# A mixture-of-experts block on one core: the experts' second layer from plain float32 to three products of split parts

## The reference

```python
T, D, I, E, K, CAP = 4096, 512, 256, 64, 6, 128
idx, w = router(x)                                # 6 of 64 experts for each token
xd = zeros((E, CAP + 1, D)).at[e_flat, slot].set(x[tok])   # up to 128 tokens for an expert
h  = square(relu(einsum('ecd,eid->eci', xd, w1)))          # first layer, 512 -> 256
yd = einsum('eci,edi->ecd', h, w2)                         # second layer, 256 -> 512
y  = zeros((T, D)).at[tok].add(yd[e_flat, slot] * gate)    # added up for each token
out = x + layernorm(shared(x) + y)
```

## Time and profile before

| | us |
|---|---|
| median of the three runs shown | 1407.62 (1406.45 to 1408.04) |
| the profiled execution, its own time | 1404.05 |
| its span | 1402.3 |
| TensorE busy, of the span | 1180.5 (84%) |
| VectorE busy | 794.6 (57%) |
| ScalarE busy | 589.5 (42%) |
| GpSimd busy | 284.0 (20%) |

### The profile page before, as it was taken

One profiled execution on the slowest core, in us unless ns is written; L12 is line 12 of the kernel. 1 busy time (PEld: TensorE's weight loads), 2 busy tenths in 40 slices (PEclk: granted clock), 3 DMA queues, 4 the chain that ended last, 5 costly groups with the idle time before them and its releaser, 6 DMA issues. The chain is left out here.

```text
span 1402.3 us, 15536 instructions
## 1 busy us (share of the span) xinstructions
PE 1180.5 (84%) x5024; PEld 773.5 (55%) x5024; DVE 794.6 (57%) x2013; ACT 589.5 (42%) x993; POOL 284.0 (20%) x278
## 2 busy tenths in 40 slices
PE   5998998989898976598989888999999999999400
PEld 3443443434343434377878776777777677777300
DVE  4689797988797989676767681122212221221036
ACT  3464565665565666432232322333333333333124
POOL 2000010201010102100000001332333333343157
PEclk9998999999999987799999998999999999999755
DMA  8201030202020232342121114987996997788997
GB/s 313 97 0 60 0 120 26 95 30 90 30 90 1 90 124 86 139 169 66 63 94 35 64 35 161 234 223 217 258 241 175 275 237 202 226 241 231 285 226 261
DMA packets 80654, 196.74 MB, mean 140 GB/s; under 512 B 10048, under 2 KB 10176, under 8 KB 79552
## 3 DMA queue, kind: packets, MB, share of 16 engines
q1 hardware_dynamic: 64128, 155.93, 33.0%
q0 software_dynamic: 16448, 39.85, 13.8%
HBM read 143.83 MB, written 51.94 MB: 140 GB/s over the span
## 5 line engine op out<-in xcount | busy, mean ns | idle before, releaser
L474 PE MATMUL bank<-mix_ring,weights 128*128 128x512 f32 x768 | 349.8, 613 | 24.7 <-ACT bank L789 15.8
L474 PEld LDWEIGHTS bank<-mix_ring,weights 128*128 128x128 f32 x768 | 149.4, 197 | 214.3 <-issue 208.2
L1560 DVE TENSOR_TENSOR run_max<-run_max 128x256 f32<-128x256 f32 x64 | 27.2, 425 | 218.2 <-ACT run_max L950 218.2
L1534 DVE TENSOR_TENSOR k_sb<-k_sb 128x512 f32<-128x512 f32 x64 | 48.1, 752 | 179.9 <-ACT k_sb L917 179.9
L1115 POOL DMA_INDIRECT ysh<-k_sb,mixf x64 | 101.6, 1588 | 197.3 <-DMA ysh<-k_sb,mixf 105.7
L481 PE MATMUL bank<-weights,rw 128*128 128x512 f32 x256 | 120.3, 626 | 21.9 <-ACT sr L753 12.4
L590 PE MATMUL bank<-h_high,ffn_w 128*128 128x512 f32 x256 | 113.8, 444 | 10.8 <-ACT k_sb L917 10.8
L1094 POOL DMA_INDIRECT xres<-h,mixf x48 | 47.9, 997 | 347.5 <-DVE mixf L1544 334.7
L917 ACT ACTIVATE k_sb<-bank 128x512 f32<-128x512 f32 x64 | 38.2, 597 | 181.3 <-PE bank L592 181.3
L607 PE MATMUL bank<-ffn_w,s_split 128*128 128x512 f32 x256 | 112.1, 438 | 0.0
L592 PE MATMUL bank<-h_high,ffn_w 128*128 128x512 f32 x256 | 101.2, 395 | 0.0
(11 more groups left out here) (210 smaller groups left out, 2057.6 us busy)
## 6 DMA issues: line engine op xcount, KB each, us to landing
wkv<-in_w SPq DMA_DIRECT2D x96, 512.0 KB, 4.4
state<-in_w SPq DMA_DIRECT2D x32, 512.0 KB, 4.4
xin<-h SPq DMA_DIRECT2D x15, 1024.0 KB, 5.6
xin<-in_x SPq DMA_DIRECT2D x8, 1024.0 KB, 5.3
xres<-in_x SPq DMA_DIRECT2D x8, 1024.0 KB, 5.3
x<-xres SPq DMA_DIRECT2D x8, 1024.0 KB, 6.6
weights<-x SPq DMA_DIRECT2D x8, 1024.0 KB, 10.9
h<-hb SPq DMA_DIRECT2D x7, 1024.0 KB, 4.3
```

The costliest lines, as they stand in the source:

```text
L474: mm = pe.matmul(bank[:, d, :], W(j)[:, ck, d * P:(d + 1) * P], mix_slot(4 * j + ck), start=(ck == 0), stop=(ck == CK - 1))
```

## The change

The second layer of an expert is computed as three products of split parts for each of its two chunks. `e_relu` on ScalarE squares the hidden values itself, rounded, as the high part `e_hi`; `e_square` on VectorE squares in place and subtracts, which gives `e_lo`. The weights are split on the fly: `w2_round(e)` on ScalarE copies w2 (128x1024) rounded into the one buffer `w2_hi`, and `w2_rest(e)` on VectorE subtracts, which gives `w2_lo` in the place of the weights themselves.

```diff
+        e_hi = [e_split[:, (2 + b) * HID:(3 + b) * HID] for b in range(2)]
+        e_lo = [e_split[:, b * HID:(b + 1) * HID] for b in range(2)]
+        w2_hi = xnd_split[:, IK * C:2 * IK * C]
+        w2_lo = [wkv_split[:, (2 * b + 1) * CK * HID:(2 * b + 2) * CK * HID] for b in range(3)] + [state_split[:, CK * HID:2 * CK * HID]]
...
             def e_second(e):
-                pe.wait_ge(S[f"w2_loaded{e % WB}"], 16 * (e // WB + 1))
-                pe.wait_ge(S["e_square"], e + 1)
+                pe.wait_ge(S["e_hi_ready"], e + 1)
+                pe.wait_ge(S["e_lo_ready"], e + 1)
+                pe.wait_ge(S["w2_hi_ready"], e + 1)
+                pe.wait_ge(S["w2_lo_ready"], e + 1)
                 if e >= 1:
                     pe.wait_ge(S["e_gated"], e)
                 for i in range(IK):
-                    mm = pe.matmul(route_bank, e_act[b][:, i, :], w2_sb[e % WB][:, i, :], start=(i == 0), stop=(i == IK - 1))
+                    pe.matmul(route_bank, act_hi[:, i, :], hi[:, i, :], start=(i == 0), stop=False)
+                    pe.matmul(route_bank, act_hi[:, i, :], lo[:, i, :], start=False, stop=False)
+                    mm = pe.matmul(route_bank, act_lo[:, i, :], hi[:, i, :], start=False, stop=(i == IK - 1))
...
             def e_relu(e):
                 act.wait_ge(S["e_up"], e + 1)
                 if e >= 2:
-                    act.wait_ge(S["e_square"], e - 1)
+                    act.wait_ge(S["e_down"], e - 1)
                 act.activation(e_hidden[e % 2], e_up_bank[:, 0:HID], ACT.Relu).then_inc(S["e_relu"], 1)
+                act.wait_ge(S["e_relu"], e + 1)
+                act.activation(e_hi[e % 2], e_hidden[e % 2], ACT.Square).then_inc(S["e_hi_ready"], 1)
+
+            def w2_round(e):
+                act.wait_ge(S[f"w2_loaded{e % WB}"], 16 * (e // WB + 1))
+                if e == 0:
+                    act.wait_ge(S["table_ready"], 4)
+                else:
+                    act.wait_ge(S["e_down"], e)
+                act.activation(w2_hi, w2_sb[e % WB].rearrange("p k c -> p (k c)"), ACT.Copy).then_inc(S["w2_hi_ready"], 1)
...
                     e_relu(0)
+                    w2_round(0)
...
                 e_gate(e)
+                if within(e, 1):
+                    w2_round(e + 1)
...
             def e_square(e):
                 b = e % 2
-                dve.wait_ge(S["e_relu"], e + 1)
-                if e >= 2:
-                    dve.wait_ge(S["e_down"], e - 1)
-                dve.tensor_tensor(e_act[b].rearrange("p k n -> p (k n)"), e_hidden[b], e_hidden[b], ALU.mult).then_inc(S["e_square"], 1)
+                dve.wait_ge(S["e_hi_ready"], e + 1)
+                dve.tensor_tensor(e_hidden[b], e_hidden[b], e_hidden[b], ALU.mult).then_inc(S["e_square"], 1)
+                dve.wait_ge(S["e_square"], e + 1)
+                dve.tensor_tensor(e_lo[b], e_hidden[b], e_hi[b].bitcast(F32), ALU.subtract).then_inc(S["e_lo_ready"], 1)
+
+            def w2_rest(e):
+                dve.wait_ge(S["w2_hi_ready"], e + 1)
+                dve.tensor_tensor(w2_lo[e % WB], w2_sb[e % WB].rearrange("p k c -> p (k c)"), w2_hi.bitcast(F32), ALU.subtract).then_inc(S["w2_lo_ready"], 1)

             def expert(e):
                 if e == 0:
                     index_scatter(0)
                     e_square(0)
+                    w2_rest(0)
                 if within(e, 1):
                     e_square(e + 1)
                     index_scatter(e + 1)
+                    w2_rest(e + 1)
                 if within(e, EB):
                     index_gather(e + EB)
```

More of the change, by code:

```diff
@@ L76, in sandwich @@
         xnd = sb("xnd", [P, CK, TT])
+        xnd_split = sb("xnd_split", [P, CK * TT], F32R, over="xnd")
         xnT = sb("xnT", [P, CK, TT + 1])
@@ L83, in sandwich @@
         run_max = sb("run_max", [P, 2, TT + 1])
+        e_split = sb("e_split", [P, 2 * (TT + 1)], F32R, over="run_max")
         state = sb("state", [P, 2, 2, TT + 1])
+        state_split = sb("state_split", [P, 4 * (TT + 1)], F32R, over="state")
         wkv = sb("wkv", [P, 12 * TT])
+        wkv_split = sb("wkv_split", [P, 12 * TT], F32R, over="wkv")
         unit = wkv[:, :].rearrange("p (b s t) -> p b s t", b=2, s=6)
@@ L120, in sandwich @@
         yout_ready ysh_stored logits_done score_ready sel_ready pos_ready placed route_step gates_ready gates_stored hots_ready tabled table_ready
-        gather_index scatter_index xd_turned xdT_ready e_up e_relu e_square e_down e_gated added
+        gather_index scatter_index xd_turned xdT_ready e_up e_relu e_hi_ready e_square e_lo_ready w2_hi_ready w2_lo_ready e_down e_gated added
         out_stored ln4_stats ln4_moments ln4_rstd o_joined o_normed o_ready o_added""".split()
@@ L212, in sandwich @@
         e_hidden = [flat_run_max[:, b * HID:(b + 1) * HID] for b in range(2)]
-        e_act = [flat_run_max[:, (2 + b) * HID:(3 + b) * HID].rearrange("p (k n) -> p k n", k=IK) for b in range(2)]
+        e_hi = [e_split[:, (2 + b) * HID:(3 + b) * HID] for b in range(2)]
+        e_lo = [e_split[:, b * HID:(b + 1) * HID] for b in range(2)]
+        w2_hi = xnd_split[:, IK * C:2 * IK * C]
+        w2_lo = [wkv_split[:, (2 * b + 1) * CK * HID:(2 * b + 2) * CK * HID] for b in range(3)] + [state_split[:, CK * HID:2 * CK * HID]]
         e_out = [k_sb[:, q // 2, 2 + q % 2, :] for q in range(EB)]
@@ L639, in e_second @@
                 b = e % 2
-                pe.wait_ge(S[f"w2_loaded{e % WB}"], 16 * (e // WB + 1))
-                pe.wait_ge(S["e_square"], e + 1)
+                act_hi, act_lo = (x[b].rearrange("p (k n) -> p k n", k=IK) for x in (e_hi, e_lo))
+                hi, lo = (x.rearrange("p (k c) -> p k c", k=IK) for x in (w2_hi, w2_lo[e % WB]))
+                pe.wait_ge(S["e_hi_ready"], e + 1)
+                pe.wait_ge(S["e_lo_ready"], e + 1)
+                pe.wait_ge(S["w2_hi_ready"], e + 1)
+                pe.wait_ge(S["w2_lo_ready"], e + 1)
                 if e >= 1:
```

## The result

| | before | after |
|---|---|---|
| median of five runs | 1407.37 (1404.50 to 1408.04) | 1429.09 (1419.29 to 1433.35) |
| ratio, 95% interval | | 1.0152 [1.0124, 1.0179] |
| profiled execution, own time | 1404.05 | 1419.29 |
| its span | 1402.3 | 1417.6 |

The change makes the kernel slower by 1.5%, some 22 us. Its five runs spread over 14 us; the five of the kernel before spread over 3.5 us, but 19 more of that one on another chip over 15 (1399.87 to 1414.58), so the wider spread need not come from the change.

A forecast was written before the change was run, and what follows sets the result against it. TensorE bounds the kernel, transfers next. Regular steps -1.9, tile changes -3.3, tile starts +11.2 and first expert +0.5 sum to +6.5 us: 1410.5 us profiled, 1414.1 us median; range 1397 to 1430.

The forecast's parts named there:

- What bounds the kernel: Stretch of 64 experts: TensorE is the bound, busy all 61.00 us; DMA engines, busy 0.90, are the next suspects.
- Prices: Per expert: TensorE 0.37 us less, w2 copy 1.05 us, w2 subtraction 1.22 us, gather issued 4.10 us after gate start.
- Regular steps: 38 intervals between gates, away from tile changes and tile starts: 6.65 us in place of 6.70, -1.9 us.
- Nine intervals around tile changes: Around the three tile changes, the gather is covered by TensorE's other work: 9 x -0.37 = -3.3 us.
- Tile starts: Three stretches of four intervals without down products between paired experts: 26.6 us each after the change, +11.2 us.
- The first expert: Waits for its own w2 copy and subtraction, 2.3 us, mostly covered by other experts' work: +0.5 us.
- The end: Behind expert 59, scatters wait for each other: nothing won, this part moves along with that expert's gate.
- gathers meet the loads: Rival: gathers fall in with weight loads, landings of 6.0 us, +24 us, 1431 us; chance 0.13.
- The first rival: TensorE stays the bound, faster, if gathers land within 4.66 us and scatters within 5.4: -14.7, 1392.9 us; chance 0.17.
- the first chain: Gate, w2 copy, w2 subtraction, index copy, gather issue: the gather leaves at the earliest 4.10 us after the gate starts.
- the second, of the scatters: Each scatter waits for the one before, 5.7 us landing plus some 0.9 to next issue: 6.6 us per expert.
- estimate of 2.7 us: Landing of a gather of 128 rows of 2304 bytes; two experts would need 10.7 us, gathers never holding TensorE up.

The follow-up runs named there:

- e8: The changed kernel with the second half of every w1 from expert 4 on not loaded; 1408.62 us, ratio 1.0017.
- e1: The changed kernel with index_gather(e+4) ahead of w2_rest(e+1) in VectorE's order, nothing else; 1411.69 us, ratio 1.0038.
- e3: The changed kernel with two buffers for w2's high part, three for w2, so the next w2 is split before the gate; 1406.43 us, ratio 0.9999.
- e12: The kernel before plus w2's copy and subtraction into a dead place, the subtraction behind index_gather; 1413.04 us, ratio 1.0042.
- e9: The changed kernel with the load of the next tile's h (1 MB) six experts later; 1428.79 us, ratio 1.0152.

## Why the prediction was right, and where it was off

*What bounds the kernel.* Right: TensorE at first, the transfers with 0.90 directly behind.

*Prices.* The 0.37 us of TensorE: an expert without waits takes 6.35 us, forecast 6.33. Copy 1.050, subtraction 1.226, as forecast. Gather 3.80 us behind the gate, forecast 4.10: the copy of w2 begins 0.58 us behind the gate's start and not after its full 0.69, and the index copy starts 1.14 us after the subtraction does.

*Regular steps.* Forecast 6.65 us per expert, measured 252.63 / 38 = 6.65. So close an agreement is partly chance: the gathers are issued 0.3 us earlier than forecast, and it is not every expert that is a little late but ten of the 38 intervals that take 7.4 us on average, while the other 28 take 6.35. The gain was -5.4 and not -1.9 us, since before they took 6.79 on average, with the late gathers that were already there, and not the 6.70 of an undisturbed one.

*Nine intervals around tile changes.* Forecast -3.3, measured -2.0. The turn of the next tile waits for `h_rest`, which now stands behind w2_rest on VectorE; I had priced only TensorE's own work there. TensorE waits 10.2 us for it instead of 7.2. That the number is still near has luck in it: before the change the clock fell behind two of the three pauses at the tile changes, in the profile after behind none.

*Tile starts.* This is the term that was mis-sized: forecast +11.2 us, measured 90.55 - 68.61 = +21.9 us. The mechanism was the one given: a tile start is two rounds of gate, gather, landing, transposes and gate, and the six rounds add up to all of the 90.55 us. From gate to issue they take 22.8 us together (forecast 6 x 4.10 = 24.6), from issue to use 38.1 (6 x 5.38 = 32.3), from use to gate 29.7 (6 x 3.83 = 23.0). The last two numbers were those of regular steps. The landing is longer where four experts' weights and rows are fetched close together (6.78 us from issue to use at 980.01), which e8 ties to the weight transfers, and it seems to the h load too. This could have been read from the trace of before: for the two gathers issued within its first tile start, between 968 and 980 us, line L1094 gives

```profile
DMA to landing us min/median/max: 6.6/7.0/7.5
```

And the lower clock behind a longer pause was left out: in four of the six rounds it takes 5.5 us from the transposes to the gate, with 3.83 assumed. That it can fall was in the trace of before as well, where behind a pause of 2.41 us, which ended at 1054.58, the granted clock was 0.53 from 1055 to 1058 us; but behind the same pause at the tile change before, which ended at 940.12, it stayed at 1.00:

```profile
940.12:943.12 3.00, 3.00 (x22) 2.64 (x23) 0.13 (x1) 0.98 (x2) 0.00 (x0) 1.00 0.18 33
...
1055.00:1058.00 3.00, 3.00 (x17) 3.00 (x16) 0.00 (x0) 0.60 (x1) 1.59 (x1) 0.53 0.07 29
```

*The first expert.* Forecast +0.5, measured 873.63 - 874.22 = -0.6 us.

*The end.* It moved along with expert 59, +14.9 at the last scatter, as forecast.

The sum: +15.2 between the two profiles with +6.5 forecast; the medians are 21.7 apart, more than three times the forecast. The direction and the mechanism were right. That the range held the time was luck: 1429.1 us is 0.9 us inside its upper end of 1430, and one of the five runs (1433.35) is beyond it. The time is outside the forecast's own range (1410 to 1423), at that of the rival "gathers meet the loads", which was right about tile starts and wrong about regular steps. The first rival's point, that moving the index ahead would leave only the products' gain, is refuted by e1: 1411.69 and not 1392.9. Behind the first chain stands the second, of the scatters, which I had priced with 6.6 us per expert only as a floor and not as what holds the gathers. The estimate of 2.7 us for such a transfer, from the Trainium skill's figures ("DMA: Bandwidth & Descriptors", on the anatomy of one DMA), describes none of these gathers, of which those with TensorE waiting for them took from 3.6 us (e8, half the bytes of w1) to 9.0 us (e3) from issue to use.

## What to carry to other kernels

When work is added to an engine with much idle time, read its queue and not its busy share: one subtraction of 1.2 us on an engine that is busy for a fifth of the time cost 17 us, since it waits for a copy behind the gate and a copy of 128 indices stood behind it. Issue what only starts a transfer ahead of anything that waits for the bound engine, and look for the slack where the work is densest, not where it is regular. And where the DMA engines are at 0.9, take a saving on the compute engine as real only once the transfers have been given an earlier start.

## What was not expected of the hardware

*GpSimd's issue of an indirect DMA is longer beside a subtraction on VectorE that began first.* In e1 a scatter's issue at 1243.76 took 2.59 us instead of the usual 1.59, beside a subtraction of two SBUF tensors from 1243.66 to 1244.89. Before the change the issues of the scatters never took more than 1.67; the third number is the longest, in ns.

```profile
L1141 POOL DMA_INDIRECT ysh<-k_sb,mixf x64: 1557/1588/2642, 875.6 to 1336.2; - x64
```

```profile
L1115 POOL DMA_INDIRECT ysh<-k_sb,mixf x64: 1557/1587/1670, 875.8 to 1332.5; - x64
```

The Trainium skill says in "SBUF — State Buffer", section on the two separate sides, that a VectorE instruction with two SBUF inputs holds the port pair that it shares with GpSimd against a GpSimd instruction that reads SBUF, and that the other one blocks. The rows agree with it, an issue longer by 1.0 us beside a subtraction of 1.23; that the port is the cause was not tried.

Which of the two began first decides. In all traces together 71 scatter issues overlap, by over 0.2 us, a subtraction of 1024 columns that had begun before them. 57 of these take more than 1.75 us; of the other 14, four began within 0.03 us of the subtraction and ten met only its last 0.2 to 0.3 us. Another 209 had begun before the subtraction did, and of these only one takes more than 1.75 us (1.79).

*Behind pauses of equal length the clock falls or stays.* A pause of 3.06 us at a tile start was followed by a granted clock of 0.68 over 3.4 us and 1.6 us more until the next gate, a pause of 0.98 us by neither. In between there is no sharp border. The shortest pause ahead of a gathered expert's transposes behind which the clock fell is one of 1.88 us (e12, 0.74 over the next 3 us), the longest behind which it stayed at 1.00 is one of 3.11 us (e9; experts 4 to 63 of all traces). The pause of 2.41 us that comes at each tile change was followed by a lower clock at two of three tile changes before the change and at none after it. So a pause of 2 to 3 us costs its own length, and in some cases 1.6 us or more on top.
